# Second attention: the transposed probabilities are stored with batch and head innermost

## The chip, the cores and the metric

The kernel runs on one core of a Trainium2 chip. The metric is the device time of one execution in microseconds (us). A core has TensorE (PE; its weight loads are listed apart as PEld), VectorE (DVE), ScalarE (ACT), GpSimd (POOL) and SyncE (SP), which here issues the DMAs. Each engine runs its own instruction stream in order; streams meet at semaphores. SBUF is the on-chip memory of 128 partitions, and PSUM holds what TensorE writes (8 banks of 512 fp32 values a partition).

## The reference

A block of three residual stages over `x` (4 batches, 128 positions, 512 features, 16 heads of 32): a cross-attention over 2048 context rows, a self-attention with relative positions, and a gated attention. The change is in the second:

```
rel = clip(r[:, None] - r[None, :], -64, 64) + 64
q, k, v = proj(Wq), proj(Wk), proj(Wv)
a_q, a_k, a_v = Eq[rel], Ek[rel], Ev[rel]
logits = (q @ k.T + q . a_k + k . a_q + a_q . a_k) * scale
attn = softmax(logits, axis=-1)
out = einsum('bhlm,bhmd->bhld', attn, v) + einsum('bhlm,lmd->bhld', attn, a_v)
x = x + out
```

Both terms of `out` contract over m, the attended position. The first takes one matrix of values for each batch and head; the second takes, for each query position l, a table of its own that all batches and heads share.

## The kernel before, in words

The order of every engine's work is written out by hand, with one semaphore wait ahead of what needs one. The names: `B = 4` batches, `C = 4` groups of heads (`u` or `hg`), `J = 4` heads in a group, `P = 128`, `HD = 32`.

In the second attention the logits of head group u stand in `s_buf`, query position l on partitions. DVE adds what was read back from DRAM (`add2`, L1304), takes the maximum (L1308), subtracts it (L1311; group 3 gives it to the exponential as a bias) and later sums the exponentials (`total2`, L1318). ACT takes the exponentials (`exp2`, L909, and L913 for group 3). PE transposes them (`attention_t`, L550), so that m is on partitions: 16 transposes for each group, four to a batch, into one PSUM bank for each batch. They are copied to SBUF, to the tensor `blocks`, one copy for each batch of [128 x 512]: by ACT for groups 0, 1 and 3 (`at_copy`, L924) and by DVE for group 2 (L1334). `blocks` is `[P, G, J, P]` and group u, batch b is block `u * B + b`, so before the change a value's place in its partition is `((u * 4 + b) * 4 + j) * 128 + l`: l is innermost.

PE reads `blocks` twice, always as the moving operand, and always with 32 stationary columns whose result goes to 32 of the 128 PSUM partitions; four neighbouring matmuls in the program take the four quarters of them in turn.

- The value product (L591): for each group, batch and head one matmul of 128 moving columns, the l of one head, neighbours in memory. 64 matmuls.
- The table product (L610): for each l one matmul with the table `ev_rel[:, l, :]` as stationary operand and 64 moving columns, the 16 pairs of group and batch by four heads at that l: 128 fp32 values (512 bytes) apart. 128 matmuls, in four banks of 32.

Matmuls here are fp32, and the trace has two weight-load records and two matmul records for each.

The order of PE's stream near the change is: `attention_t(0)`, logits of group 3 (L526 and L531), `attention_t(1)`, `attention_t(2)`, projections of the values of batches 2 and 3 (`values2`, L341), `attention_t(3)`, the value product, bank 0 of the table product, the transposes back (`attended_t`, L599), banks 1 to 3 of the table product. `values2(2, 0)` may not start before the first copy of `at_copy(1)` has read its bank; `attention_t(3)` takes each batch as ACT's exponentials of group 3 are done; the value product waits for ACT's two copies of the values (`values2`, L904), then group by group for the copies of the probabilities, for group 3 batch by batch.

ACT's order is: `at_copy(0)`, `exp2(2)`, a weight conversion (`weight_hi(4)`, L750), `at_copy(1)`, `exp2(3)`, two copies of values (L904), `at_copy(3)`, the four copies of the value product's result to `k_t` (L950), `weight_hi(5)`. After the table product DVE transposes its result out of PSUM (`ev_transpose`, L1352, which waits for all four banks), POOL scales it (L1102), DVE adds it to `x_res` (L1358) and takes the moments for the next layer norm. POOL's scaling stands behind `weight_lo(5)` (L1044), which waits for `weight_hi(5)`.

Two other places of the same kernel have strided access. The logits product (L531) reads both operands from `q_lb` and `k_lb`, where b is innermost: 128 columns, 16 bytes apart, 32 stationary rows to a matmul. The copies that fill these two tensors (`keys2` L890 and `queries2` L894, ACT) write 512 values 16 bytes apart. The third attention keeps the layout that the second has before the change (copies L986, product L682), and the first attention's value product (L429) reads moving columns 8 bytes apart.

Of the kernel before, what the change touches and what calls it, by code (L numbers as in the profile page):

```python
# [12 lines left out]
P = 128  # L13
B = 4
D = 512
C = D // P
H = 16
HD = D // H
J = P // HD
G = B * C  # L20
# [17 lines left out]
def program(nc, a, out):  # L38

    with ExitStack() as ctx:  # L40
        def sb(name, shape, dt=F32):
            return ctx.enter_context(nc.sbuf_tensor(name, shape, dt))

        def sem(name):
            return ctx.enter_context(nc.semaphore(name))
# [9 lines left out]
        blocks = sb("blocks", [P, G, J, P])  # L55
# [34 lines left out]
        ps = ctx.enter_context(nc.psum_tensor("ps", [P, 8, 512], F32))  # L90
# [48 lines left out]
        ring = blocks[:, :].rearrange("p g j q -> p (g j q)")  # L139
# [40 lines left out]

        def lg3(u):
            return s_buf[:, 0, u * H:(u + 1) * H, :]

        def probs_t(u):
            return blocks[:, u * B:(u + 1) * B]
# [17 lines left out]
        s = {n: sem(n) for n in names}  # L203
# [99 lines left out]
        def _(pe):  # L303
# [135 lines left out]
            for hg in range(C):  # L439
                for c in range(C):  # L440
                    last = mm(ps[:, hg, :], wq_raw[:, c, hg * P:(hg + 1) * P], x_t0[:, c, :],  # L441
                              start=c == 0, stop=c == C - 1)
# [4 lines left out]
               stop=True).then_inc(s["pos_psum"], 1)  # L447
# [133 lines left out]
            for hg in range(C):  # L581
                if hg < 2:
                    pe.wait_ge(s["at_done"], B * (hg + 1))
                elif hg == 2:
                    pe.wait_ge(s["at_dve"], B)
                for b in range(B):
                    if hg == C - 1:
                        pe.wait_ge(s["at_done"], 2 * B + b + 1)
                    for j in range(J):
                        part = slice((hg * J + j) * HD, (hg * J + j + 1) * HD)  # L590
                        last = mm(ps[j * HD:(j + 1) * HD, b, hg * P:(hg + 1) * P], v_buf[:, 1, b, part],  # L591
                                  probs_t(hg)[:, b, j, :], start=hg == 0, stop=hg == C - 1, skip_group_check=True)
                    if hg == C - 1:
                        last.then_inc(s["av2"], 1)

            def attended_t(b):
                pe.wait_ge(s["av2_evac"], b + 1)
                for hg in range(C):
                    last = nc.tensor.transpose(ps[:, b, hg * P:(hg + 1) * P], k_t[:, b, hg * P:(hg + 1) * P], ident[:])  # L599
                last.then_inc(s["av2_t"], 1)  # L600

            pe.wait_ge(s["ev_in"], 16)
            for bank in range(4):
                if bank == 1:
                    for b in range(B):
                        attended_t(b)
                for n in range(8):
                    for i in range(4):
                        l = i * HD + bank * 8 + n
                        last = mm(ps[i * HD:(i + 1) * HD, 4 + bank, n * 64:(n + 1) * 64], ev_rel[:, l, :],  # L610
                                  blocks[:, :, :, l].rearrange("p (u b) j -> p b u j", u=C), start=n == 0, stop=n == 7,
                                  skip_group_check=True)
                last.then_inc(s["ev2"], 1)

# [48 lines left out]
            def attention3_t(u):  # L663
                pe.wait_ge(s["exp3"], u + 1)
                for b in range(B):
                    if u == 0:
                        pe.wait_ge(s["v3_done"], b + 1)
                    else:
                        pe.wait_ge(s["at3_done"], B * (u - 1) + b + 1)
                    for j in range(J):  # L670
                        last = nc.tensor.transpose(ps[:, 4 + b, j * P:(j + 1) * P], lg3(u)[:, b * J + j, :], ident[:])
                    last.then_inc(s["at3_psum"], 1)
# [67 lines left out]
        def _(act):  # L740
            copy = nc.scalar.copy
# [175 lines left out]
            def at_copy(u):  # L917
                base = 0 if u < 2 else 4
                if u == 0:
                    for n in range(SLOTS):  # L920
                        act.wait_ge(s[f"rel_out_{n}"], 16 * len(range(n, NROUND, SLOTS)))
                for b in range(B):
                    act.wait_ge(s["at_psum"], B * u + b + 1)
                    copy(probs_t(u)[:, b], ps[:, base + b, :].rearrange("p (j l) -> p j l", j=J)).then_inc(s["at_done"], 1)  # L924

            keys2(0)
            queries2(0)
# [10 lines left out]
            exp2(1)  # L938
            values2(1, 1)
            at_copy(0)  # L940
            exp2(2)
            weight_hi(4)
            at_copy(1)
            exp2(3)
            values2(2, 0)
            values2(3, 1)
            at_copy(3)
            for b in range(B):
                act.wait_ge(s["av2"], b + 1)
# [23 lines left out]
            def exp3(u):  # L973
                act.wait_ge(s["sub3"], u + 1)
                if u >= SUMS:
                    nc.scalar.activation(lg3(u), lg3(u), ACT.Exp, scale=SCALE).then_inc(s["exp3"], 1)
                    return
                for n in range(H):
                    last = nc.scalar.activation(lg3(u)[:, n, :], lg3(u)[:, n, :], ACT.Exp, scale=SCALE,
                                                accum_out=rsum[:, u * H + n:u * H + n + 1])  # L980
                last.then_inc(s["exp3"], 1)
# [133 lines left out]
        def _(dve):  # L1115
# [215 lines left out]
            softmax2(3)  # L1331
            for b in range(B):
                dve.wait_ge(s["at_psum"], 2 * B + b + 1)
                nc.vector.tensor_copy(probs_t(2)[:, b],  # L1334
                                      ps[:, 4 + b, :].rearrange("p (j l) -> p j l", j=J)).then_inc(s["at_dve"], 1)
            for u in range(1, C):
                total2(u)
# [203 lines left out]
```

## Time and profile before

| | us |
|---|---|
| median of 3 runs | 781.33 (780.76 to 782.13) |
| the profiled execution | 777.19 |
| its span | 775.2 |
| PE busy | 716.6 (92%) |
| DVE busy | 631.5 (81%) |
| ACT busy | 482.3 (62%) |
| POOL busy | 499.8 (64%) |

PE records overlap each other, since matmuls are pipelined, so the mean duration of one is longer than the distance between two: the pace of a run of matmuls is its length divided by its count. The stretch that the change touches lies between 650 and 690 us of the span. The span's first 590 us are the first attention, the last 85 the third stage.

### The profile page before, as it was taken

How to read it: one execution, taken by the hardware profiler on the slowest of the kernel's cores; microseconds unless marked ns; L12 is line 12 of the kernel's file. 1: busy time of each engine (PE TensorE's matmuls, PEld its weight loads, DVE VectorE, ACT ScalarE, POOL GpSimd, SP SyncE). 2: the span in 40 equal slices, each digit the busy share in tenths (PEclk: the TensorE clock that was granted, in tenths of full speed). 3: DMA queues.
4: the chain of work that ended last, by engine and by line, in shares of the span. 5: the costliest groups of instructions: out<-in, count | busy, mean ns of one | idle time of the engine just before them, and what ended most of it. 6: DMA issues, size and time to landing. Idle time of an engine off the chain costs nothing.

```text
span 775.2 us, 16946 instructions
## 1 busy us (share of the span) xinstructions
PE 716.6 (92%) x7394; PEld 552.2 (71%) x7394; DVE 631.5 (81%) x509; ACT 482.3 (62%) x686; POOL 499.8 (64%) x280
## 2 busy tenths in 40 slices
PE   4988999999999999999999999999388998939988
PEld 2566777777777777777777777777275677837877
DVE  4349999999999999999999999999985359775685
ACT  4458686676866768667686676866623454813681
POOL 0044879798898988989889898897952020433300
PEclk9999999999999999999999999999788999979999
DMA  8110101101011010110101101011013999220101
GB/s 318 58 55 1 56 1 56 54 3 56 1 56 55 3 56 2 55 56 2 56 1 56 56 1 56 2 55 46 11 55 121 334 393 381 97 96 0 57 2 54
DMA packets 15337, 55.68 MB, mean 72 GB/s; under 512 B 1696, under 2 KB 2080, under 8 KB 11680
## 3 DMA queue, kind: packets, MB, share of 16 engines
q1 hardware_dynamic: 15264, 54.61, 19.2%
q8 instruction: 58, 0.95, 0.5%
q14 instruction: 15, 0.12, 0.0%
HBM read 43.13 MB, written 11.47 MB: 70 GB/s over the span
## 4 chain that ended last, share of the span: by engine, by line
PE 81%; DVE 9%; DMA 4%; ACT 3%; issue 2%; SPq 0%; POOL 0%; ACTq 0%; DVEq 0%; POOLq 0%
PE ps L341 27%; PE ps L324 25%; PE ps L398 9%; PE ps L429 8%; DMA rel_scratch<-blocks 3%; PE ps L441 2%; PE ps L332 2%; PE ps L360 1%; PE ps L610 1%; DMA s_buf<-rel_scratch 1%; PE ps L350 1%; PE ps L504 1%; DVE blocks L1294 1%; DVE s_buf L1204 1%; DVE stats L1119 1%
## 5 line engine op out<-in xcount | busy, mean ns | idle before, releaser
L1061 POOL TENSOR_TENSOR s_buf<-s_buf,r_all 128x1024 f32<-128x1024 f32 x93 | 197.2, 2161 | 0.9 <-DVE r_all L1224 0.9
L781 ACT COPY s_buf<-ps 128x1024 f32<-128x1024 f32 x128 | 123.1, 1016 | 11.4 <-PE ps L398 11.4
L797 ACT ACTIVATE s_buf<-s_buf 128x1024 f32<-128x1024 f32 x128 | 130.1, 1056 | 0.0
L1182 DVE TENSOR_REDUCE extra<-s_buf 128x128 f32<-128x2048 f32 x48 | 109.5, 2281 | 22.5 <-ACT s_buf L781 22.5
L1044 POOL TENSOR_TENSOR w_lo<-raw,w_hi 128x2048 fp32r<-128x2048 f32 x8 | 37.0, 4631 | 114.5 <-ACT w_hi L750 74.0
L1204 DVE TENSOR_TENSOR s_buf<-s_buf,ps 128x2048 f32<-128x2048 f32 x49 | 109.1, 2282 | 0.5
L773 ACT COPY v_buf<-ps 128x512 f32<-128x512 f32 x64 | 37.5, 585 | 92.5 <-PE ps L341 92.5
L1033 POOL TENSOR_TENSOR v_buf<-v_buf,extra 128x512 f32<-128x512 f32 x64 | 82.1, 1310 | 13.3 <-ACT v_buf L773 13.3
L429 PE MATMUL ps<-s_buf,v_buf 128*32 128x128 f32 x2048 | 73.4, 283 | 13.7 <-DVE s_buf L1232 9.6
L1039 POOL TENSOR_TENSOR odd_lo<-raw,odd_hi 128x512 fp32r<-128x512 f32 x32 | 40.4, 1291 | 65.1 <-ACT odd_hi L758 65.1
L398 PEld LDWEIGHTS ps<-q_t,k_t 32*128 32x128 f32 x2048 | 63.0, 186 | 25.5 <-issue 25.5
L429 PEld LDWEIGHTS ps<-s_buf,v_buf 128*32 128x32 f32 x2048 | 55.6, 110 | 35.7 <-issue 26.5
L1211 DVE TENSOR_REDUCE extra<-s_buf 128x128 f32<-128x2048 f32 x32 | 73.0, 2282 | 9.3 <-ACT s_buf L797 9.3
L1211 DVE TENSOR_REDUCE ps<-s_buf 128x128 f32<-128x4096 f32 x16 | 70.8, 4427 | 9.8 <-ACT s_buf L797 9.8
L398 PE MATMUL ps<-q_t,k_t 32*128 32x128 f32 x2048 | 75.1, 283 | 2.7 <-ACT k_t L765 2.7
L765 ACT ACTIVATE k_t<-ps,cols 128x512 f32<-128x512 f32 x64 | 44.1, 688 | 50.9 <-PE ps L324 50.9
L1055 POOL TENSOR_TENSOR s_buf<-s_buf,m_all 128x2048 f32<-128x2048 f32 x15 | 62.0, 4133 | 2.5 <-DVE m_all L1197 2.5
L341 PE MATMUL ps<-w_hi,x_hi 128*128 128x512 f32 x176 | 53.1, 424 | 3.7 <-ACT k_t L765 3.7
L1039 POOL TENSOR_TENSOR x_lo<-raw,x_hi 128x512 fp32r<-128x512 f32 x28 | 35.3, 1292 | 21.7 <-ACT x_hi L758 21.7
L341 PE MATMUL ps<-w_lo,x_hi 128*128 128x512 f32 x176 | 48.1, 396 | 0.0
L341 PE MATMUL ps<-w_hi,x_lo 128*128 128x512 f32 x176 | 47.3, 391 | 0.0
L1182 DVE TENSOR_REDUCE ps<-s_buf 128x128 f32<-128x2048 f32 x16 | 36.8, 2297 | 8.0 <-ACT s_buf L781 6.4
(193 smaller groups left out, 1404.6 us busy)
## 6 DMA issues: line engine op xcount, KB each, us to landing
raw<-in_ctxT SPq DMA_DIRECT2D x16, 1024.0 KB, 4.9
rel_scratch<-blocks SPq DMA_DIRECT2D x16, 636.0 KB, 10.7
s_buf<-rel_scratch SPq DMA_DIRECT2D x7, 1210.0 KB, 9.7
raw<-in_Wk SPq DMA_DIRECT2D x2, 1024.0 KB, 4.8
raw<-in_Wq SPq DMA_DIRECT2D x2, 1024.0 KB, 6.8
raw<-in_Wv SPq DMA_DIRECT2D x2, 1024.0 KB, 5.8
extra<-in_EvRel SPq DMA_DIRECT2D x1, 2048.0 KB, 13.0
extra<-rel_scratch SPq DMA_DIRECT2D x1, 1210.0 KB, 9.6
```

Of the source, the lines that this page charges most:

```text
L324: last = mm(ps[:, bank, :], w_parts[v][:, slot, c, hg * P:(hg + 1) * P], x_parts[u][:, c, :], start=n + c == 0, stop=n == 2 and c == C - 1)
L341: last = mm(ps[:, bank, :], x_parts[u][:, c, b * P:(b + 1) * P], w_parts[v][:, slot, c, :], start=n + c == 0, stop=n == 2 and c == C - 1)
L398: last = mm(pair, k_t[rows, w, keys], q_t[rows, w, keys], start=True, stop=True, skip_group_check=True)
L429: last = mm(ps[j * HD:(j + 1) * HD, bank, b * P:(b + 1) * P], v_of(t)[:, b, h * HD:(h + 1) * HD], probs[:, j, b // 2, :, b % 2], start=b = ...
L781: copy(piece(t, 2 * w + u).rearrange("p e (u n) -> p (e u) n", u=2), ps[:, 2 * u:2 * u + 2, :]).then_inc(s["s_evac"], 1)
L797: nc.scalar.activation(piece(t, p), piece(t, p), ACT.Exp).then_inc(s["exp_done"], 1)
L1033: pool.tensor_tensor(v, v, bv_all, ALU.add).then_inc(s["v_ready"], 1)
L1039: pool.tensor_tensor(lo[:, :, rows], raw[:, :, rows], hi[:, :, rows], ALU.subtract).then_inc(s["ctx_lo"], 1)
L1061: pool.tensor_tensor(part, part, spread(r_all, 4), ALU.mult).then_inc(s["attn_pool"], 1)
L1182: nc.vector.tensor_reduce(m_ps if k == 0 else m_next[:, k % 2, :], over_pairs(t, 2 * k, 2), AX.XY, ALU.max).then_inc(s["max_done"], 1)
L1204: tt(part, part, m_wide.broadcast_to([P, 8, P, 2]), ALU.subtract).then_inc(s["sub_dve"], 1)
L1211: nc.vector.tensor_reduce(r_ps if k == 0 else z_next[:, k % 2, :], over_pairs(t, p, n), AX.XY, ALU.add).then_inc(s["sum_done"], 1)
```

## The change

`rows_of_l` is a new view of the same memory as `blocks`, with l outermost and head innermost: a value's place is now `l * 64 + b * 16 + u * 4 + j`. The twelve copies by ACT and the four by DVE write their 512 values there through `probs2(u)`: in the order in which they run over j and l, two neighbours are 64 values (256 bytes) apart. The value product reads its 128 columns 256 bytes apart. The table product reads its 64 columns as 64 neighbours, in another order of b and u than that of memory before, but the same order of columns. The third attention keeps `probs_t`. No instruction is added, removed or moved on any engine, nor is any wait.

```diff
+        rows_of_l = ring[:, 0:G * J * P].rearrange("p (l b u j) -> p l b u j", b=B, u=C, j=J)
+
+        def probs2(u):
+            return rows_of_l[:, :, :, u].rearrange("p l b j -> p b j l")
...
                         last = mm(ps[j * HD:(j + 1) * HD, b, hg * P:(hg + 1) * P], v_buf[:, 1, b, part],
-                                  probs_t(hg)[:, b, j, :], start=hg == 0, stop=hg == C - 1, skip_group_check=True)
+                                  probs2(hg)[:, b, j, :], start=hg == 0, stop=hg == C - 1, skip_group_check=True)
...
                         last = mm(ps[i * HD:(i + 1) * HD, 4 + bank, n * 64:(n + 1) * 64], ev_rel[:, l, :],
-                                  blocks[:, :, :, l].rearrange("p (u b) j -> p b u j", u=C), start=n == 0, stop=n == 7,
+                                  rows_of_l[:, l].rearrange("p b u j -> p (b u j)"), start=n == 0, stop=n == 7,
...
-                    copy(probs_t(u)[:, b], ps[:, base + b, :].rearrange("p (j l) -> p j l", j=J)).then_inc(s["at_done"], 1)
+                    copy(probs2(u)[:, b], ps[:, base + b, :].rearrange("p (j l) -> p j l", j=J)).then_inc(s["at_done"], 1)
...
-                nc.vector.tensor_copy(probs_t(2)[:, b],
+                nc.vector.tensor_copy(probs2(2)[:, b],
                                       ps[:, 4 + b, :].rearrange("p (j l) -> p j l", j=J)).then_inc(s["at_dve"], 1)
```

## Rows read from the trace of the kernel before

**Rows 1.** Chain of waits, 655 to 684 us: start, length, what, count.

```profile
655.88 2.30 DVE s_buf L1304
...
658.32 1.94 PE ps L550 x16
...
660.27 5.74 PE ps L341 x24
666.00 1.75 PE ps L550 x16
667.75 3.63 PE ps L591 x128
671.38 2.59 PE ps L610 x61
673.97 1.90 PE ps L599 x16
675.87 7.15 PE ps L610 x158
...
683.04 0.73 DVE v_buf L1352
```

**Rows 2.** Timeline of PE: start, length, engine, line; the products that read `blocks`.

```profile
667.68 3.70 PE L591 MATMUL ps<-blocks,v_buf 128*32 128x128 f32 x128
...
671.20 2.77 PE L610 MATMUL ps<-blocks,extra 128*32 128x64 f32 x64
...
675.80 7.20 PE L610 MATMUL ps<-blocks,extra 128*32 128x64 f32 x192
```

**Rows 3.** Timeline of PE: other short products, strided and not.

```profile
313.77 1.12 PE L429 MATMUL ps<-s_buf,v_buf 128*32 128x128 f32 x32
...
653.55 2.26 PE L531 MATMUL ps<-v_buf,k_t 32*128 32x128 f32 x32
...
735.58 1.17 PE L659 MATMUL ps<-k_t,s_buf 32*128 32x128 f32 x32
...
753.05 1.08 PE L682 MATMUL ps<-blocks,v_buf 128*32 128x128 f32 x32
```

**Rows 4.** One line each (L591, L610, L531): min, median, max ns of a record.

```profile
L591 PE MATMUL ps<-blocks,v_buf x128: 272/273/298, 667.7 to 671.1; 128*32 128x128 f32 x128
L610 PE MATMUL ps<-blocks,extra x256: 287/335/346, 671.2 to 682.7; 128*32 128x64 f32 x128
L531 PE MATMUL ps<-v_buf,k_t x128: 404/411/597, 627.8 to 655.4; 32*128 32x128 f32 x128
```

**Rows 5.** Timeline of DVE and POOL, 674 to 684 us.

```profile
674.67 0.70 DVE L1344 TENSOR_TENSOR ps<-ps,rinv 128x512 f32<-128x512 f32 x1 [4.41 <-PE ps L599]
674.84 4.93 POOL L1044 TENSOR_TENSOR w_lo<-raw,w_hi 128x2048 fp32r<-128x2048 f32 x1 [9.43 <-ACT w_hi L750]
...
679.40 0.70 DVE L1346 TENSOR_TENSOR x_res<-ps,x_res 128x512 f32<-128x512 f32 x1
```

**Rows 6.** Windows: length, busy time of PE, PEld, DVE, ACT, POOL, PEclk, DMA share, GB/s.

```profile
675.80:683.05 7.25, 7.20 (x193) 6.87 (x192) 4.20 (x8) 0.26 (x1) 3.96 (x1) 1.00 0.02 5
```

**Rows 7.** Groups of instructions by line: busy and mean ns of the copies.

```profile
L924 ACT COPY blocks<-ps 128x512 f32<-128x512 f32 x12 | 6.1, 601 | 0.9 <-PE ps L550 0.9
L894 ACT COPY k_t<-ps 128x512 f32<-128x512 f32 x4 | 4.3, 1075 | 10.2 <-PE ps L332 10.2
L1334 DVE COPY blocks<-ps 128x512 f32<-128x512 f32 x4 | 2.5, 681 | 0.0
```

**Rows 8.** Timeline of ACT, 657 to 668 us.

```profile
657.83 1.90 ACT L750 CAST w_hi<-raw 128x2048 fp32r<-128x2048 f32 x1 [3.47 <-DMA raw<-in_Wq]
...
659.63 2.04 ACT L924 COPY blocks<-ps 128x512 f32<-128x512 f32 x4
...
661.54 4.80 ACT L913 ACTIVATE s_buf<-s_buf,rmax 128x128 f32<-128x128 f32 x16
...
666.24 1.06 ACT L904 COPY v_buf<-ps 128x512 f32<-128x512 f32 x2
```

## The prediction

> **What bounds the kernel now.** I read the chain of waits first, because the page puts 81% of it on PE. From the end of `add2(3)` to DVE's first transpose of the table product's result the chain is PE alone [rows 1]: transposes, value projections, transposes, the value product (L591, 3.63 us), bank 0 of the table product (L610, 2.59), the transposes back, and the other three banks (7.15). Whatever changes the pace of L591 or L610 moves the end of the kernel, and what ACT does counts only where it comes to stand ahead of PE. Then the timeline of PE gives the pace of these runs, and that of ACT shows how much room it has.
>
> The paces, as distance between records (length less one record's duration, over the count less one): L591 with 128 neighbouring columns, (3.70 - 0.273) / 127 = 27.0 ns. L610 with 64 columns 512 bytes apart, (7.20 - 0.335) / 191 = 35.9 ns [rows 2, 4]. Half the columns and a third more time, with the same weight load form of 32 columns by 128 rows. Neither the load nor the issue of a record can be what makes L610 slower, since L591 does both every 27.0 ns. What is left is the stride of its moving operand. The other strided product says the same: L531, 128 columns 16 bytes apart, goes at (2.26 - 0.411) / 31 = 59.6 ns, where the third attention's logits, same shape with neighbours (L659), take 1.17 us for the same 32 records against 2.26 [rows 3, 4]. A stride of 8 bytes costs nothing to speak of: L429 takes 1.12 us and L682, without a stride, 1.08 [rows 3].
>
> **The change part by part.** Instructions and waits stay in number and order; four things change their price.
>
> (a) The value product, now 128 columns 256 bytes apart. There is no such row. From L610, price by the column: 35.9 x 128 / 64 = 71.8 ns a record. From L531, which has 128 strided columns but runs in row groups with a strided stationary operand too: 59.6 ns. Lower bound 35.9, L610's own pace, if the price were by the matmul. Since L610 is 128*32 as this one is but may have a fixed part that shorter streams feel more, I take the middle of 59.6 and 71.8, 66 ns. 128 records x (66 - 27) = +5.0 us; the two rows give +4.2 and +5.7, the lower bound +1.1. All of it is on the chain.
>
> The Trainium skill (page "SBUF — State Buffer", section "Specifications (TRN2)") has a rule that speaks against this half of the change: SBUF has lines of 16 bytes, and an access needs at least two hits on a line to go at full bandwidth. It gives no price. By it a stride of 256 bytes is no worse than one of 16 and no better than one of 512, and 8 bytes are free, which is how the four rows above stand. If the rule priced the lines alone, with no fixed part, (a) would be +5.7.
>
> (b) The table product, now 64 neighbours. L591 is an upper bound on its pace (same load, twice the columns): 27.0 ns. A lower bound is half of that, if columns alone set the pace: 13.5. I take 27.0, because no row shows matmul records closer to each other than 26 ns (L682, 32 records in 1.08 us [rows 3]). Before it takes 671.20 to the transposes' start at about 673.9, and 675.80 to 683.04, together 9.9 us [rows 1, 2]; after, 256 x 27.0 = 6.9. So -3.0 us. At 13.5 it would be 3.5 us, but then DVE takes over: its eight multiplications and additions begin 0.7 us after the transposes back begin and end at 680.10, 6.2 us after [rows 5], and `ev_transpose` stands behind them, where now it comes 9.1 after. So the lower end is -2.0 (bank 0: 2.7 to 0.9, rounded) and -2.9 (the rest), -4.9 in all. The upper end is 0.
>
> The same skill (page "TensorEngine Tiling (Array Packing)", section "Instruction Overhead") says that a matmul of one column takes as long as one of some 60. The clock granted here is 1.00 of the full 2.4 GHz [rows 6]. As an estimate from that page, 60 cycles are 25 ns a record, 6.4 us for the 256, and (b) would be -3.5; it speaks against the lower end.
>
> (c) ACT's twelve copies, whose stores are now 256 bytes apart. The nearest row is L894, same size and source, stores 16 bytes apart: 1075 ns against 601 [rows 7]. I take the difference, 0.47 us each, 1.9 for four; between 0 and, should distance matter, twice that. `at_copy(0)` (+1.9) pushes `exp2(2)`, and both are hidden by the 3.47 us in which ACT waits for Wq3 before 657.83 [rows 8]. `at_copy(1)` is not: its first copy releases `values2(2, 0)` 0.5 later, and its last ends 1.9 later, so `exp2(3)` ends at 668.2 instead of 666.3, and the two copies of values at 669.2 instead of 667.3. The value product waits for these; before it began at 667.68, PE being the later one. Now ACT is: `attention_t(3)` for the last batch can start at 668.2 and ends at 668.7, and the product starts at 669.3. So +1.6 us; 0 if strided stores are free. `at_copy(3)` then runs 669.3 to 673.2; the product wants it after the 96 records of groups 0 to 2, at 669.3 + 6.3 = 675.6, so it is hidden by (a), and would bound the product's end at 673.4 (+2.3 against 671.1) if (a) were nothing.
>
> (d) DVE's four copies: 681 ns each [rows 7], no strided store of DVE in the trace. Between 0 and ACT's +0.47, 1.9 in all. They start at 660.6 and are wanted when the product reaches group 2, after 672: hidden. The sums behind them end at most 1.9 after 669.7, and what needs them starts after the transposes back: hidden.
>
> Sum: +1.6 (c) +5.0 (a) -3.0 (b) = +3.6 us. Is anything else late? POOL's `weight_lo(5)` follows ACT's `weight_hi(5)`, which follows the copies to `k_t`: with the value product ending at 677.8, some 6.7 later than 671.1, it runs from about 681.4 to 686.4 instead of from 674.84 to 679.77 [rows 5]. `ev_transpose(0)` comes at 683.04 + 3.6 = 686.6 and POOL's scaling at 687.5. Just hidden, by 1.1 us. After that point everything shifts as one, the rest of the chain waits for no DMA that was issued before.
>
> The profiled execution took 777.19, 4.14 below the median of the runs shown (781.33). By the sum it would be 780.8; I add the same 3.6 to the median: 784.9.
>
> **The rivals.**
>
> R1, the table product gains nothing (35.9 ns has a cause that I have missed, such as 64-column streams). Then (b) is 0 and the sum is +6.6: 787.9. Against it: L591's 27.0 with the same loads.
>
> R2, strided stores or reads at 256 bytes are dearer than at 16: copies at twice the extra, `exp2(3)` another 1.9 later. Then +5.5: 786.8. For it: nothing in the trace has stores so far apart. Against it: L610's reads at 512 bytes cost per column (0.56 ns) about what L531's at 16 do (0.47).
>
> R3, nearly no change: the table product at the column rate (-4.9) and the value product at L531's 59.6 ns (+4.2), with +1.6: +0.9, 782.2. For it: the columns of L591 alone could account for its 27.0 ns, so that no floor is seen. Against it: no row has a closer pace than L682's 26.
>
> R4, faster: the stride is paid once for a matmul and not by the column. The value product then goes at 35.9 and could end at 669.3 + 4.6 = 673.9, close to where `at_copy(3)` would let it; that is +2.8 with the later start, and the table product gives -3.0 to -4.9: -0.2 to -2.1, so 779.2 to 781.1. It decides for faster from a table pace of about 19 ns. For it: one width alone of a strided 128*32 product is in the trace. Against it: L531 at twice L610's columns takes 1.7 times its pace.
>
> **How the numbers follow.** Within 0.2% (1.6 us) is what a measurement of this kernel can't tell from no change. Forecast 784.9 with its own range of 783 to 787: 0.58. R1: 0.12, R2: 0.12, both slower. R3: 0.10, half of it within the 1.6 us and half above. R4: 0.08, of which 0.05 is faster and 0.03 the same. The rest of faster, 0.01, and some of same come from the forecast's edge. Slower 0.86, same 0.08, faster 0.06. The range of 8 in 10 reaches down into R3 and up to R1: 782.5 to 788.0.
>
> **What the profile after would show.** L591 with a pace near 66 ns, so about 8.4 us for 128 records, and its matmul records longer than 273 ns. L610 with a pace near 27, 192 records in 5.2 us. L924 at about 1075 ns, `exp2(3)` ending 1.9 us later than 666.3 and the value product starting 1.6 later. DVE's L1352 3.6 us later than 683.04, and nothing different after it but the shift. I am wrong if L591 is below 40 ns, if L610 stays at 36, if ACT's copies stay at 600 ns, or if POOL's L1102 begins after `weight_lo(5)` with DVE done before it.

## The result: the changed kernel is 5.3 us slower

| | before | changed |
|---|---|---|
| median of 6 runs each, us | 780.62 (779.64 to 782.13) | 785.96 (784.96 to 787.82) |
| ratio | | 1.007, 95% interval 1.0052 to 1.0089 |
| profiled execution / its span | 777.19 / 775.2 | 787.82 / 785.9 |

The two profiled executions lie 10.6 us apart, at the fast end of the one kernel and the slow end of the other. So I compare from a mark: the start of `add2(3)` on DVE, at 655.88 before [rows 1] and 659.97 in the changed kernel. Of what the change touches only ACT's `at_copy(0)` stands ahead of it, and PE's wait that leads to the mark ends with the read-back from DRAM. The mark also lies at 658.8 to 659.9 in e2, e3 and e12, which are the kernel before up to this point (e12 but for its padding), so its 4.1 us are not the change's. From the mark to DVE's first transpose of the table product's result the kernel before takes 27.16 us (683.04), the changed one 33.16 (693.13): +6.0. A second profile of the changed kernel gives 658.60 to 691.65, 33.05: +5.9. From there to the end of the span it is 92.2 us before and 92.8 and 92.4 in the two profiles of the changed kernel, so the rest is shifted to within 0.6 us. That the medians differ by 5.3 and not by 6 is not explained: a profile is one execution.

The timeline of the changed kernel (start, length, engine, line; L596 is the value product, L591 before; L615 the table product, L610 before), answering to [rows 2]:

```profile
672.71 12.81 PE L596 MATMUL ps<-blocks,v_buf 128*32 128x128 f32 x124 [0.23 <-ACT v_buf L909]
...
685.43 1.30 PE L615 MATMUL ps<-blocks,extra 128*32 128x64 f32 x61
...
686.66 1.97 PE L604 MATMUL ps<-ident,k_t 128*128 128x128 f32 x16
...
688.55 2.87 PE L615 MATMUL ps<-blocks,extra 128*32 128x64 f32 x187
...
692.77 0.31 PE L615 MATMUL ps<-blocks,extra 128*32 128x64 f32 x5 [1.35 <-issue]
...
693.13 1.31 DVE L1357 STREAM_TRANSPOSE v_buf<-ps 128x512 f32<-128x512 f32 x2 [0.29 <-PE ps L615]
```

The value product takes 12.7 us instead of 3.5, by the starts of its records 99 ns a record instead of 27 (12.1 us and 93 ns in the second profile). The table product takes (2.87 - 0.22) / 186 = 14 ns a record instead of 36, but stops for 1.35 us ahead of its last five records, with nothing that it waits for. By the terms of the sum, each measured between starts in the two timelines:

| term | predicted | measured | second profile (e8) |
|---|---|---|---|
| start of the value product after the mark | +1.6 | 12.74 for 11.80: +0.9 | 13.46: +1.7 |
| value product | +5.0 | 12.72 for 3.52: +9.2 | 12.13: +8.6 |
| table product, without the transposes inside it | -3.0 | 5.81 for 9.94: -4.1 | 5.56: -4.4 |
| sum | +3.6 | +6.0 | +5.9 |

The copies and the sums beside the product, answering to [rows 7] (groups by line: busy, mean ns; the reduce is `total2`, 2277 ns before):

```profile
L929 ACT COPY blocks<-ps 128x512 f32<-128x512 f32 x12 | 11.1, 1075 | 2.1 <-PE ps L555 2.1
L1339 DVE COPY blocks<-ps 128x512 f32<-128x512 f32 x4 | 3.9, 1105 | 0.0
L1323 DVE TENSOR_REDUCE rsum<-s_buf 128x16 f32<-128x2048 f32 x4 | 17.5, 4420 | 0.0
```

and the minimum, median and maximum of that reduce:

```profile
L1323 DVE TENSOR_REDUCE rsum<-s_buf x4: 2258/2277/10866, 656.5 to 672.8; 128x16 f32<-128x2048 f32 x4
```

The copies cost what was forecast. The one reduce that lies beside the value product takes 10.9 us instead of 2.3 (9.5 in the second profile). It reads `s_buf`, which nobody else touches then, so it is not a value that it waits for; that it lacks access to SBUF is argued from this. Its result is wanted at 687.4, and it and the reciprocal are done at 684.5, so this cost nothing.

The chain of waits, answering to [rows 1], shows that what leads to the value product is now ACT (start, length, what):

```profile
653.22 8.28 DMA raw<-in_Wq
...
661.52 1.90 ACT w_hi L755
663.43 3.72 ACT blocks L929 x4
667.14 4.57 ACT s_buf L918 x16
671.71 0.96 ACT v_buf L909 x2
...
672.71 12.56 PE ps L596 x80
```

From the landing of Wq on, ACT has no pause: conversion, `at_copy(1)`, exponentials, two copies of values, product. The start of the value product therefore goes by when that transfer lands: 1.55 us after the mark here, 2.29 in the second profile, 1.95 before. Counted from the landing, the product starts 11.16 to 11.34 us later in all six profiles with stores one value at a time (the two of the changed kernel, e4 to e7), and 9.85 to 9.91 in the seven with the short copies where ACT waits for Wq (the kernel before, e1, e2, e3, e9, e10, e12). So the slower copies cost +1.3 here (+1.5 in e7), and not +1.6; the other 0.4 between +1.3 and +0.9 is an earlier landing. [rows 1] shows PE alone ahead of the product; in fact both paths met there, since `values2(2, 0)` begins at 660.27, when the first of ACT's copies from 659.63 on is done.

### The profile page after: what moved, and what is told of

It reads as the page before. It is cut to its first block, busy times and chain, and to the rows that moved or that the text cites. A ratio compares the mean times of both kernels' runs of the same rounds, so it can differ in the third digit from the quotient of the medians.

```text
span 785.9 us, 16946 instructions
## 1 busy us (share of the span) xinstructions
PE 723.1 (92%) x7394; PEld 554.1 (71%) x7394; DVE 642.0 (82%) x509; ACT 488.3 (62%) x686; POOL 499.8 (64%) x280
## 4 chain that ended last, share of the span: by engine, by line
PE 79%; DVE 7%; DMA 5%; ACT 5%; issue 3%; SPq 0%; POOL 0%; ACTq 0%; DVEq 0%; POOLq 0%
PE ps L346 26%; PE ps L329 24%; PE ps L403 9%; PE ps L434 8%; DMA rel_scratch<-blocks 4%; PE ps L446 2%; PE ps L596 2%; PE ps L337 2%; PE ps L365 1%; PE ps L355 1%; DMA raw<-in_Wq 1%; DVE s_buf L1209 1%; PE ps L509 1%; DVE blocks L1299 1%; ACT k_t L770 1%
## 5 line engine op out<-in xcount | busy, mean ns | idle before, releaser
L778 ACT COPY v_buf<-ps 128x512 f32<-128x512 f32 x64 | 37.5, 586 | 92.4 <-PE ps L346 92.4
L434 PE MATMUL ps<-s_buf,v_buf 128*32 128x128 f32 x2048 | 75.2, 288 | 13.1 <-DVE s_buf L1237 8.9
L434 PEld LDWEIGHTS ps<-s_buf,v_buf 128*32 128x32 f32 x2048 | 57.2, 112 | 35.3 <-issue 25.9
```

The source lines that it names most:

```text
L434: last = mm(ps[j * HD:(j + 1) * HD, bank, b * P:(b + 1) * P], v_of(t)[:, b, h * HD:(h + 1) * HD], probs[:, j, b // 2, :, b % 2], start=b = ...
```

## The experiments

The open question was why 99 ns and not 60 to 72, and what a layout would do that pays neither price. Every experiment is timed against runs of the kernel before on the same chip (medians 781.17 for e1 to e4, 780.59 for e5 to e8, 781.54 for e9 to e12). "Local" is the time from the mark to DVE's first transpose, less the 27.16 us of before. It still contains when Wq lands, 1.55 to 2.44 us after the mark (1.95 before), so two such numbers can differ by up to 0.9 us for that alone.

**e1, l kept in pairs.**

```
+        pairs_of_l = ring[:, 0:G * J * P].rearrange("p (h b u j v) -> p h b u j v", b=B, u=C, j=J, v=2)
+        def probs2(u, b):
+            return pairs_of_l[:, :, b, u].rearrange("p h j v -> p j h v")
...   value product: probs2(hg, b)[:, j]; table product: pairs_of_l[:, l // 2, :, :, :, l % 2]
```

> The changed kernel with l kept in pairs: a value's place is (l // 2) * 128 + (b, u, j) * 2 + l % 2, so the value product reads runs of two neighbours (8 bytes) 512 bytes apart, the table product 64 columns 8 bytes apart, and the copies store runs of two. Theory A, a stream pays when it takes only one fp32 value from a 16-byte line, and pays nothing when it takes two: value product back at 26 to 28 ns a record (3.5 us), table product near 15 ns, copies near 600 ns, so about 4 us below the kernel before (776.5 for 780.6). Theory B, what is paid is distance (each jump of hundreds of bytes costs, however long the run): value product at 45 to 60 ns a record, and a time between the kernel before and the changed one.

778.01 us, ratio 0.996 (0.9947 to 0.9974): 3.2 us below the kernel before; local -2.6.

```profile
L929 ACT COPY blocks<-ps 128x512 f32<-128x512 f32 x12 | 6.3, 617 | 1.5 <-DMA rel_scratch<-blocks 1.5
...
L1339 DVE COPY blocks<-ps 128x512 f32<-128x512 f32 x4 | 2.5, 680 | 0.0
```

```profile
671.90 4.84 PE L596 MATMUL ps<-blocks,v_buf 128*32 128x128 f32 x128
676.54 1.15 PE L615 MATMUL ps<-blocks,extra 128*32 128x64 f32 x64
...
679.52 3.01 PE L615 MATMUL ps<-blocks,extra 128*32 128x64 f32 x187
...
683.86 0.31 PE L615 MATMUL ps<-blocks,extra 128*32 128x64 f32 x5 [1.33 <-issue]
```

Theory A holds for the copies (617 and 680 ns, as before the change), for the reduces (all 2.3 us) and for the table product ((3.01 - 0.22) / 186 = 15 ns). The value product goes at (4.84 - 0.31) / 127 = 36 ns: far from 99, but not back at 27. Something is left, which e9 takes up.

**e2, only the value product strided, at 16 bytes.**

```
-  probs_t(hg)[:, b, j, :]
+  probs_t(hg)[:, b].rearrange("p j l -> p (j l)").rearrange("p (l j) -> p j l", j=J)[:, j]
```

> The kernel before with one thing changed: the value product reads its 128 columns 16 bytes apart inside the block that it read before (so the values are the wrong ones, and the output is not the reference's). Stores, table product and all waits are as before. If the price goes by the line (theory A), the product takes as long at 16 bytes as at 256: about 96 ns a record while VectorE's sums run beside it, 12 us, and the sum beside it is stretched from 2.3 to some 8 to 11 us: +8 to +9 us. If the distance of 256 bytes was what made it 96 and not 60 to 72 (theory B), then 60 to 72 ns, 8 to 9 us, and +4.5 to +6 us.

785.24 us, ratio 1.0047 (1.0029 to 1.0065); local +4.0. The product reads the wrong values here, as the table product does in e3 and both do in e4; the instructions and their sizes are the same. Theory B was right, if somewhat below its 60 to 72 ns: (7.55 - 0.41) / 127 = 56 ns, and all reduces beside it at 2.27 us.

```profile
672.14 7.55 PE L591 MATMUL ps<-blocks,v_buf 128*32 128x128 f32 x128
```

**e3, only the table product on neighbours.**

```
-  blocks[:, :, :, l].rearrange("p (u b) j -> p b u j", u=C)
+  ring[:, l * 64:l * 64 + 64]
```

> The kernel before with one thing changed: the table product reads 64 neighbours, a slice of the old layout (wrong values, so the output is not the reference's). Stores and value product as before. By the profile of the changed kernel the table product falls from 35.9 to about 15 ns a record; with the gap of 1.35 us that its last five records had there, the end of the table product comes 4 us earlier. VectorE's eight additions and multiplications end 6.2 us after the transposes back begin, which caps it at 4.9. So -3.5 to -4.9 us. If the gap is due to code arriving late for a faster engine, it is seen here too, in about the same size.

777.42 us, ratio 0.996 (0.9943 to 0.9977); local -3.6. The table product goes at 14 ns a record, and the gap is there too, at the same record:

```profile
677.52 2.87 PE L610 MATMUL ps<-blocks,extra 128*32 128x64 f32 x187
...
682.03 0.31 PE L610 MATMUL ps<-blocks,extra 128*32 128x64 f32 x5 [1.65 <-issue]
```

**e4, only the stores strided, at 16 bytes**, with the same rearrangement of `probs_t(u)[:, b]` as the copies' output.

> The kernel before with one thing changed: the sixteen copies store their 512 values 16 bytes apart inside their own block, and both products read as before (other values, so the output is not the reference's). By the prediction +1.6 us, from the value product's later start; in the profile of the changed kernel that start was only 0.9 us later against the end of the chain before it. The copies at about 1070 ns on ScalarE and 1100 ns on VectorE in either case. If distance mattered to stores, they would be shorter here than there (1064 and 1106).

782.60 us, ratio 1.0027 (1.0015 to 1.0038); local +2.0: a later start of the product (+1.6, of which 0.2 is a later landing of Wq), and another wait of 0.44 us, where a value product of 27 ns a record reaches group 3 before the slower `at_copy(3)` is done.

```profile
671.73 3.48 PE L591 MATMUL ps<-blocks,v_buf 128*32 128x128 f32 x120 [0.22 <-ACT v_buf L904]
...
675.65 0.43 PE L591 MATMUL ps<-blocks,v_buf 128*32 128x128 f32 x8 [0.44 <-ACT blocks L924]
```

The copies take 1150 ns (ACT) and 1079 (DVE) at 16 bytes, 1075 and 1105 at 256, 1142 and 1127 at 260 (e7): to stores, distance matters by 7% at most, and 256 bytes are not the dear ones.

**e5, the changed kernel with the sums held back:** `+ dve.wait_ge(s["av2"], B)` ahead of `total2(1)` to `total2(3)`.

> The changed kernel with VectorE's three last sums of exponentials (total2 of groups 1 to 3) held back until the value product is done. The time as a whole grows, since the scaling now waits for the sums; what is looked at is the pace. If the value product was slow (96 ns a record) because it and the sum took turns at the same memory, it goes at 60 to 72 ns here, about 8.5 us, and the sums take 2.3 us each. If the stride alone sets 96 ns, it stays there, and only the sums recover.

794.7 us in one run. The value product is what it was, to the last digit of the row, and the sums recover:

```profile
674.12 12.81 PE L596 MATMUL ps<-blocks,v_buf 128*32 128x128 f32 x124 [0.23 <-ACT v_buf L909]
...
687.30 6.67 DVE L1323 TENSOR_REDUCE rsum<-s_buf 128x16 f32<-128x2048 f32 x3 [18.17 <-PE ps L596]
```

So TensorE held back VectorE, and not the reverse. Nor is it ACT's strided stores that make the stream slow: the last copy of `at_copy(3)` ends at 677.6, and from there to 685.3 neither ACT nor DVE does anything, while the product's last 64 records still go at 90 ns and the 32 ahead of them at 106 (by their starts). The price belongs to the stream alone; why its pace falls along the way, and why the second profile has 93 ns, was not found.

**e6, heads innermost:** place `u * 2048 + b * 512 + l * 4 + j`, so the value product and the stores go at 16 bytes and the table product reads runs of four.

> A third layout, with the four heads of a group innermost: place u * 2048 + b * 512 + l * 4 + j. The value product and the copies go at 16 bytes, the table product reads runs of four neighbours (16 bytes) 2048 bytes apart. If the price goes by the line, this is the changed kernel over again: value product at 90 to 100 ns, table product near 15, time within 1 us of it. If 256 bytes is a bad distance, value product at 60 to 72 and 3 to 4 us faster than the changed kernel. If runs of a whole line are not enough for the table product, it stays near 36 and the kernel is 4 us slower than the changed one.

782.16 us, ratio 1.0018 (1.0004 to 1.0031), 3.8 below the changed kernel's median; local +1.3. Value product (7.58 - 0.41) / 127 = 56 ns, table product (3.08 - 0.22) / 186 = 15 ns, from runs of four values 2048 bytes apart. Beside this table product some of DVE's additions are longer than their usual 0.69 us, and they are what ends last; all eight end 6.05 us after the first begins, where the changed kernel has 5.42.

```profile
669.48 7.58 PE L596 MATMUL ps<-blocks,v_buf 128*32 128x128 f32 x128 [0.22 <-ACT v_buf L909]
...
680.92 1.19 DVE L1351 TENSOR_TENSOR x_res<-ps,x_res 128x512 f32<-128x512 f32 x1
```

**e7, 260 bytes in place of 256:** 65 values from one l to the next, in a `blocks` that is 512 bytes longer.

> The changed kernel with 65 values from one l to the next in place of 64 (260 bytes, no power of two), everything else the same. If 256 bytes makes neighbours in the stream meet in the same bank, the value product falls from 96 to 60 to 72 ns a record, and the time by 3 to 4 us. If it is one value from each line that costs, nothing changes, within 1 us.

782.22 us, ratio 1.0019 (1.0006 to 1.0032), 3.7 below the changed kernel; local +1.2. With everything else the same, four bytes more take the value product from 99 to (7.63 - 0.41) / 127 = 57 ns, and the three reduces beside and ahead of it from 15.23 to 6.63 us:

```profile
668.83 6.63 DVE L1325 TENSOR_REDUCE rsum<-s_buf 128x16 f32<-128x2048 f32 x3
...
674.03 7.63 PE L598 MATMUL ps<-blocks,v_buf 128*32 128x128 f32 x128 [0.23 <-ACT v_buf L911]
```

**e8, the changed kernel again.**

> The changed kernel once more, unaltered, for a second profile: value product 12.6 us, table product at 15 ns a record with a gap of some 1.4 us before its last records if that gap belongs to the code and not to chance, the third of the sums stretched to 11 us.

785.97 us in one run; value product from 672.06 to about 684.2, 93 ns a record and so somewhat faster than in the first profile, the longest reduce 9.5 us and not 11, gap 1.32 us at the same record.

**e9, pairs at 520 bytes in place of 512:** e1 with 130 values from one pair of l to the next.

> The kernel with l in pairs (e1_pairs) and 130 values from one pair of l to the next in place of 128, so that the value product's runs of two are 520 bytes apart and not 512. In e1_pairs the value product went at 36 ns a record and not at 27. If that rest was the power of two, it falls to 27 here, 1.1 us, and the table product, which reads 8 bytes apart as before, stays at 16: about 4.2 us below the kernel before. If runs of two cost something in themselves, 36 ns stays and the time is that of e1_pairs.

778.26 us, ratio 0.9953 (0.9939 to 0.9967); local -3.5, 0.9 better than e1; in the medians against the runs of before on the same chip, 3.3 and 3.2, e1 and e9 can't be told apart. The value product falls from 36 to (4.16 - 0.28) / 127 = 31 ns, not to 27: most of the rest was the power of two, some of it is the run of two.

```profile
672.54 4.16 PE L598 MATMUL ps<-blocks,v_buf 128*32 128x128 f32 x128
```

**e10, TensorE's code moved by 16 instructions:** `+ for n in range(4): mm(ps[0:HD, 7, 0:1], ident[:, 0:HD], ident[:, 0:1], ...)` in e1, ahead of `logits(0)`.

> e1_pairs with 4 tiny fp32 matmuls (16 instructions) added on TensorE ahead of logits(0), where it waits for the read-back from DRAM, into a bank that is overwritten next. Every instruction behind them lies 16 places later in TensorE's code. If the gap of 1.3 us that stands 187 records into the last three banks of the table product is TensorE waiting for a page of its code, it moves 8 records forward, to 179 and 13. If it belongs to the end of the product or to a semaphore, it stays at 187 and 5.

777.16 us in one run. The gap moved by 8 records, as 16 instructions of two to a record say:

```profile
678.93 2.89 PE L617 MATMUL ps<-blocks,extra 128*32 128x64 f32 x179
...
682.83 0.43 PE L617 MATMUL ps<-blocks,extra 128*32 128x64 f32 x13 [1.01 <-issue]
```

**e11, moved by 240 instructions:** 60 such matmuls in e9.

> e9_pairs_130 with 60 such tiny matmuls (240 instructions) ahead of logits(0). In pages of 256 instructions the page border that fell 374 instructions into the last three banks (of 384) falls 134 in, and the one after it behind the product's end. If the gap is a page of code that comes late because the page before it was used up in 1.9 us, it is gone or under 0.3 us, since the page before the new border holds the slower transposes; the product ends 1 to 1.3 us earlier, less what then waits for VectorE's additions (they end 6.2 us after the transposes back begin), so -0.3 to -1 us against e9. The 60 matmuls lie in a wait of several us and cost nothing.

780.08 us, ratio 0.9986 (0.9972 to 1.0): slower than e9. Half right. The gap is gone, and now DVE's additions end last, at 684.75. Its local -4.3 is the best of all, but not by the gap: Wq has landed before ACT asks for it, and the value product starts 11.53 us after the mark and not 12.34 as in e9, which is the whole difference of 0.8. From the transposes back to DVE's transpose it is 6.1 us, and 6.3 in e9: the gap was worth 0.2, as the cap by DVE's additions says.

The 60 matmuls were not free. They take 4.27 us in all, 32 ns a record by the starts of the first hundred, and TensorE had only 0.33 us to wait there in e9. They end 2.8 us after the time at which the transposes of the first logits (L533) began in e9. These transposes then take 3.68 us for 1.94: the granted clock, 1.00 while the first 100 or so of the small records ran, is 0.50 from 631.6 to 638.4, and 1.00 throughout 628 to 636 in e9. Together the first logits (L538) come at 636.04 where they came at 631.53. That the small matmuls brought the clock down was not tried; the kernel before has such a dip too, 3.4 us long, a little later, at 632.3.

```profile
628.23 4.27 PE L573 MATMUL ps<-ident 128*32 128x1 f32 x120
632.43 3.68 PE L533 MATMUL ps<-ident,s_buf 128*128 128x128 f32 x16
636.04 2.26 PE L538 MATMUL ps<-v_buf,k_t 32*128 32x128 f32 x32
...
680.47 3.14 PE L619 MATMUL ps<-blocks,extra 128*32 128x64 f32 x192
...
684.06 0.69 DVE L1355 TENSOR_TENSOR x_res<-ps,x_res 128x512 f32<-128x512 f32 x1
```

The stretch with the transposes as a window (length, busy time of PE, PEld, DVE, ACT, POOL, PEclk, DMA share, GB/s):

```profile
632.50:636.00 3.50, 3.50 (x17) 3.21 (x16) 0.00 (x0) 0.00 (x0) 2.30 (x1) 0.50 1.04 404
```

**e12, the kernel before with the table product at 516 bytes:** 129 values from one head to the next.

> The kernel before with 129 values from one head's l to the next in place of 128: the table product's 64 columns are 516 bytes apart and not 512, all else equal (value product and copies contiguous). The strided value product went at 57.5 ns for 128 columns at 16 and at 260 bytes, 0.449 ns a column, and the table product at 512 bytes at 35.9 for 64, 0.56 a column. If distance at a power of two is part of that, the table product falls to 28.7 ns a record, 1.8 us in all; if a 64-column stream has a fixed part instead, it stays at 35.9.

780.47 us, ratio 0.9988 (0.9979 to 0.9997); local -1.4, or -1.75 from the landing of Wq. (6.05 - 0.302) / 191 = 30 ns where it was 36. The kernel before paid the power of two as well, in the row from which I had the price.

```profile
678.83 6.05 PE L611 MATMUL ps<-blocks,extra 128*32 128x64 f32 x192
```

The paces together, ns a record of 128*32 matmuls:

| distance of the runs | values in a run | columns | ns a record | ns a column |
|---|---|---|---|---|
| neighbours (before, e3, e12) | 128 | 128 | 27 | 0.21 |
| neighbours (changed, e3) | 64 | 64 | 14 | 0.22 |
| 16 bytes (e2, e6) | 1 | 128 | 56 | 0.44 |
| 260 bytes (e7) | 1 | 128 | 57 | 0.44 |
| 256 bytes (changed; second profile) | 1 | 128 | 99; 93 | 0.77; 0.73 |
| 512 bytes (before) | 1 | 64 | 36 | 0.56 |
| 516 bytes (e12) | 1 | 64 | 30 | 0.47 |
| 512 bytes (e1) | 2 | 128 | 36 | 0.28 |
| 520 bytes (e9) | 2 | 128 | 31 | 0.24 |

All these stretches ran at a granted clock of 1.00. What four or eight bytes of padding take away is nearly the same for each run at 512 bytes in e12 (6 ns for 64 runs, 0.09 each) and in e9 (5 ns for 64, 0.08 each), and much more at 256 (42 ns for 128 runs, 0.33 each).

## Why the prediction held, and where it was off

The direction and the mechanism were right, and the time, 785.96, lies in the stated range and 1.1 us above the forecast. That it is so near is in part luck. The value product alone missed by 4.2 us, more than the whole forecast change of 3.6; the table product gained 1.1 more than forecast and the start cost 0.7 less, which leaves +6.0. The medians then moved by 5.3 only, and the forecast was added to 781.33, where six runs of the kernel before have 780.62. R2's time, 786.8, is even a little nearer than the forecast's.

(a) The value product was mis-sized: 66 ns taken, with 59.6 and 71.8 as ends; 99 measured (93 in the second profile), +9.2 us and not +5.0. The step that failed is the reading of L610 as a price "by the column" that could be carried to another distance. L610 contained a second price that I did not separate, since both strided rows of the trace had one distance each: without it L610 goes at 30 ns (e12), by the column 60 for this product, and the 57 that a distance of 260 bytes costs is near that. What 256 bytes cost on top stood in no row. At 16 and at 260 bytes the product goes at 56 and 57 ns (e2, e6, e7), close to L531's 59.6: one value from each 16-byte line. At 256 bytes another 42 ns come on top, which four bytes of padding take away. I had written that by the line rule "a stride of 256 bytes is no worse than one of 16". The rule itself, 16-byte lines and two hits for full bandwidth (the Trainium skill, "SBUF — State Buffer", "Specifications (TRN2)"), fits what was measured: 56 and 57 ns with one value from a line at either distance (e2, e7), and 36 and 31 with two (e1, e9), though not quite 27. The conclusion that distance then does not matter is not in it, was mine, and is wrong.

(b) The table product was mis-sized the other way: 27 ns taken, 14 measured, which is close to the lower end of 13.5 that I had called unlikely. Half the columns take half the time, so L591's 27 ns were set by its 128 columns, and not by a floor of some 26 ns for any record. The cap was right: DVE's additions end at 692.84, 6.2 us after the transposes back begin, and with the gap of 1.35 us TensorE is just 0.3 us later. So the gap costs 0.3 us of its 1.35. The Trainium skill ("TensorEngine Tiling (Array Packing)", "Instruction Overhead") speaks of the latency of one matmul; my estimate of 25 ns took it as the pace of a stream, and the measurement decides against that: 64 columns with a new weight load go at 14 ns a record in column groups of 32.

(c) The stores: 0.47 us more for each of ACT's copies, as forecast, and the path through `exp2(3)` to the value product is the one that the chain shows. Four of them in a row take 3.81 us for 2.04, so +1.8 and not +1.9, and counted from the landing of Wq the product starts 1.3 us later, not 1.6. What I had left out is that the start follows this landing: +0.9, +1.7 and, in e4, +1.6 against the mark differ by that. The hidden parts stayed hidden. (d) DVE's copies took 1105 ns, within the bounds, hidden. What I had not seen is the reduce of 10.9 us, which happened to have 2.9 us of room.

POOL's `weight_lo(5)` ran from 688.68 to 693.24 and its scaling began at 693.99, hidden as said, by 0.75 us and not 1.1.

The rivals: R1 is out by the table product's 14 ns. R3 and R4 are out by the value product's 99: the table product's half of R3, close to the column rate, came nearly true. R2 named reads or stores at 256 bytes that are dearer than at 16, and priced the stores. The stores are not dearer (e4), the reads are, so its mechanism was half right.

## What to carry to other kernels

When two readers want different orders of one fp32 tensor, don't give one of them neighbours and the other single values: try to interleave so that both take runs of two. Here that beats the kernel before, and so the changed one: by 0.4% (e1), and 0.47% with the rows padded off the power of two (e9), which the times do not tell apart, for neither a copy nor an instruction more. Before pricing a strided operand from another row, ask what distance that row has; a price taken from one distance is not a price by the element.

## What was not expected of the hardware

- A strided stream of TensorE at 256 bytes slows VectorE's sum over another tensor from 2.3 to 10.9 us (9.5 in the second profile); the same stream at 16, at 260 or in pairs at 512 bytes leaves it at 2.3 (e2, e7, e1), and it is itself not slowed by it (e5). Runs of four at 2048 bytes go with additions of up to 1.19 us for 0.69 (e6); this was seen once and not isolated.
- TensorE stops as if it ran out of code. In all kernels with a fast table product it stops for 0.9 to 1.65 us after the same number of records, and 16 instructions added earlier move the stop by exactly 8 records (e10). With 240 added it is gone (e11). At 36 and at 30 ns a record there was no such stop. That the stop goes with a place in the instruction stream is shown; that TensorE waits there for its code is argued, since the trace names nothing that it waits for.
- A 128*32 matmul record of one column took 32 ns at a granted clock of 1.00 (e11), more than one of 64 neighbouring columns with 14. All 60 of those used the same quarter of the array, those of the table product the four in turn. That this is the reason was not tried.
- Why the distance costs was not settled either. 256 and 512 bytes were tried against a distance 4 or 8 bytes longer; 16 bytes are a power of two as well and cost no more than 260. Nothing between 16 and 256 was tried, nor any single values further apart than 516.
